# A decoder layer on one core: new first and last batches of the attention, and a closing stage whose loads are issued in the stage before it

## The chip, the cores and the metric

One core of one Trainium2 chip runs the whole program in one launch. The metric is the device time of one execution in microseconds (us), the median of several. A profile is taken of one execution; its span runs from the first to the last recorded work, and the execution's own time is a little longer than its span.

## What is computed

The input is x with 8 batches of 256 tokens of 512 features, float32, and a context of the same shape. Three residual blocks follow one another:

```
x = x + attention(layernorm(x))      # 16 heads of 32; each query sees 26 first and 64 last keys
x = x + convolution(ctx, ctx, layernorm(x))   # causal convolution of products of the context
x = x + ffn(layernorm(x))            # 12 experts, each token goes to its best 3
# ffn, closing part, for each batch:
#   pooled = mean over the 256 tokens of the experts' sum
#   phi    = sigmoid(relu(pooled @ Wp1 + bp1) @ Wp2 + bp2)
#   out    = sum * (1 - 0.8 * (phi > 0.7))
```

## The kernel before, in words

The kernel is five stages one after the other: attention, convolution, route, experts, finish. Each stage is a block with its own program for every engine, and a stage starts when all engines have left the one before. Inside a stage the order of work on an engine is written out by hand, and engines wait for each other on counted semaphores. TensorE is called PE below, VectorE is DVE, ScalarE is ACT, GpSimd is POOL, SyncE is SP.

**Attention.** A tile is 128 tokens, and a batch has two (t = 0, 1). All of x stays in SBUF as `xs`. SP loads x in four quarters of 1 MB each (L214), then the four weight matrices of 1 MB (L216), then small tables. ACT issues the load of the constants and, right behind it, those of the four biases. DVE computes the layer norm's statistics of all 16 tiles (L384, L387), ACT takes a square root (L231), DVE inverts it, and only then `normalise(0, 0)` starts (L403), whose result PE transposes (L528). Projections of batch 0 follow (L551). `kp`, the taps of the convolution, gets its diagonal from DVE after `add_bias(0, 3)`, is written out by SP, and ACT waits for that (`pad_out`) before it begins `batch(0)`.

`batch(b)` is software-pipelined: on PE it is scores of tile 0 (L571), projections of batch b+1, transposes of the probabilities `p_t` (L579), scores of tile 1, `p_v` (L592), the output product `w_o` (L560), and so on; transposes of the second layer norm's result of batch b-1 (`n_t`) lie between. ACT computes the exponentials, one instruction for each head (L258), and evacuates PSUM: `evac_pt` (L267), `evac_o` (L276), `evac_n` (L272). DVE does the row maxima (L423), the division of the probabilities (L433), biases, residual and statistics. The scores of tile 1 write the same four PSUM banks as those of tile 0 and the transposed probabilities, so they wait until tile 0 is through. In the last batch there is nothing of a next batch to fill the gaps; the order is otherwise the same.

**Experts.** 59 tiles of 128 gathered tokens go through two products. ACT scales a tile's result into `y` (L1548), POOL adds the expert's bias (L1478), copies the tile's indices (L1480), executes three short instructions that let earlier ones settle (L1455), and issues an indirect DMA that adds `y` into `acc` in DRAM (L1488). POOL waits for the last of these before the stage may end. SP loads the experts' weights, and at its end `x2`, the residual.

**Finish.** SP issues eight loads of `acc` into `o` (L1684), one per batch; ACT issues loads of the gate's weights. PE sums each batch over its tokens by a product with a column of ones, `pool_half(h)` for four batches (L1723), with two products per batch, one for each tile; the trace counts two MATMUL records for each float32 product here. Then the gate, `gate_half(h)`: transposes (L1730), hidden layer (L1736), output (L1742), with ACT and DVE between. PE does half 0's sums and gate, then half 1's. DVE then multiplies and adds the residual, eight instructions per half (L1770), and SP stores a batch when its two are done (L1688).

Of the kernel before, what the change touches and what calls it, by code (L numbers as in the profile page):

```python
# [14 lines left out]
P = 128  # L15
B, S, D = 8, 256, 512
KD = D // P
# [79 lines left out]
def attention(nc, xs, cst, x, wqT, wkT, wvT, woT, bq, bk, bv, bo, consts, qe, taps, diag, kpad):  # L97

    with ExitStack() as ctx:
# [35 lines left out]
        power = sb("power", [P, TPB])  # L135
# [5 lines left out]
        ps_t = psum("ps_t", [P, 512])  # L141
        ps_p = psum("ps_p", [P, 2, 512])
        ps_s = psum("ps_s", [P, 4, 512])
        ps_o = psum("ps_o", [P, KD, P])

        x_in = [sem(f"x_in{i}") for i in range(4)]
# [17 lines left out]
        pt_evac = sem("pt_evac")  # L164
        pv_done = sem("pv_done")
# [45 lines left out]
        def _(sp):  # L211
            xt = x.rearrange("b (t p) d -> p (b t) d", p=P)
            for i in range(4):
                sp.dma_start(xs[:, 4 * i:4 * i + 4, :], xt[:, 4 * i:4 * i + 4, :]).then_inc(x_in[i], 16)  # L214
            for w, src, s in ((wq, wqT, wq_in), (wk, wkT, wk_in), (wv, wvT, wv_in), (wo, woT, wo_in)):
                sp.dma_start(w[:].rearrange("p (k n) -> p k n", k=KD),  # L216
                             src.rearrange("(k p) n -> p k n", p=P)).then_inc(s, 16)
# [8 lines left out]
        def _(act):  # L226
            act.dma_start(cst[:], consts).then_inc(c_in, 16)
            for t, src in ((bias_q, bq), (bias_k, bk), (bias_v, bv), (bias_o, bo)):
                act.dma_start(t[:], src.partition_broadcast(P)).then_inc(b_in, 16)
            act.wait_ge(var_ready, 1)  # L230
            nc.scalar.activation(rstd[:], rstd[:], ACT.Sqrt).then_inc(std_ready, 1)  # L231
# [22 lines left out]
            def exps(b, t):  # L254
                for f in range(2):
                    act.wait_ge(nmx_ready, 4 * b + 2 * t + f + 1)
                    for s in range(8 * f, 8 * f + 8):
                        last = nc.scalar.activation(pm[:, t, s * NK:(s + 1) * NK],  # L258
                                                    ps_s[:, s // 4, (s % 4) * NK:(s % 4 + 1) * NK], ACT.Exp,
# [49 lines left out]
            batch(B - 1, True, False, True)  # L309
            evac_n(B - 1)  # L310

        @block.gpsimd
        def _(pool):
# [29 lines left out]
            def inverse_std(b):  # L343
                pool.wait_ge(var1_ready, b + 1)
                nc.gpsimd.tensor_tensor(rstd1[:], rstd1[:], power[:], ALU.pow).then_inc(rstd1_ready, 1)
# [18 lines left out]
            pool.wait_ge(power_ready, 1)  # L364
            pool.wait_ge(c_in, 16)
            first = Steps(pool, pool_step)
            for j in range(3):
                rope(0, j, first)
            batch(0, False, False)
# [9 lines left out]
        def _(dve):  # L379

            for i in range(4):
                dve.wait_ge(x_in[i], 16)
                with dve.Fori(4 * i, 4 * i + 4) as t:
                    nc.vector.bn_stats(stats[:, t], xs[:, t]).then_inc(stats_done, 1)  # L384
            dve.wait_ge(stats_done, NT)
            for t in range(NT):
                nc.vector.bn_aggr(mv[:, t], stats[:, t]).then_inc(aggr_done, 1)  # L387
            dve.wait_ge(aggr_done, NT)
            steps = Steps(dve, dve_step)
            nc.vector.tensor_scalar(rstd[:], mv[:, :, 1], EPS, None, ALU.add).then_inc(var_ready, 1)  # L390
            dve.wait_ge(std_ready, 1)
            steps.do(nc.vector.reciprocal(rstd[:], rstd[:]))
            dve.wait_ge(b_in, 64)
# [25 lines left out]
            def softmax_top(b, t, steps):  # L419
                dve.wait_ge(s_done, 2 * b + t + 1)  # L420
                for f in range(2):
                    sc = view(ps_s[:], f * 1024, [[512, 2], [NK, 4], [1, NK]])
# [4 lines left out]
            def softmax_sum(b, t, steps):  # L427
                for f in range(2):
# [78 lines left out]
            batch(B - 1, True, False, True, tail)  # L507
# [5 lines left out]
        def _(pe):  # L513
# [50 lines left out]
            def scores(b, t):  # L564
# [1312 lines left out]
```

## Time and profile before

| | us |
|---|---|
| median of 3 runs | 1565.55 |
| lowest, highest | 1563.95, 1566.26 |
| the profiled execution's own time | 1563.66 |
| its span | 1561.5 |
| what lies around the span | 2.2 |

The profile's times count from the start of the span. PE is the busiest engine with 1396.8 us. Busy time of another engine matters only where PE, or the end of the program, waits for it.

### The profile page before, as it was taken

To read this page: it belongs to the slowest core of one execution; us is meant where nothing else is said; L and a number is where in the kernel's file an instruction comes from. 1 tells how busy PE (TensorE), PEld (TensorE's weight loads), DVE (VectorE), ACT (ScalarE), POOL (GpSimd) and SP (SyncE) were. 2 spreads that over 40 slices of the span, in tenths; PEclk is the share of its full clock that TensorE was granted. 3 is DMA by queue.
4 is the path that set the end of the run, shared out by engine and by line. 5 is a ranking of instruction groups with operands and counts; after the bars stand their busy time and mean duration, and the time that the engine had idled before them with its cause. 6 is when DMAs were issued, how large, how long until landed. Compare 5 with 4: busy or idle time off the path is not lost. (4 is left out here: it accounts for less than half of the span.)

```text
span 1561.5 us, 27353 instructions
## 1 busy us (share of the span) xinstructions
PE 1396.8 (89%) x7656; PEld 1080.8 (69%) x7657; DVE 783.9 (50%) x1075; ACT 680.7 (44%) x1847; POOL 862.8 (55%) x989
## 2 busy tenths in 40 slices
PE   3899999769999526999999999999999999999956
PEld 1455555447777315888888888888888888888842
DVE  3455665539999687474434717446462552000003
ACT  0555555523444422444444444444444444445420
POOL 1544445324456305767676767767676766656530
PEclk9999999879999757999999999999999999999987
DMA  7000000015333333554444535444453543332115
GB/s 254 3 1 0 0 0 1 1 43 208 94 112 111 142 141 102 128 158 111 114 102 106 144 68 144 122 121 121 127 140 74 136 110 71 86 89 34 27 32 217
DMA packets 75461, 148.20 MB, mean 95 GB/s; under 512 B 9056, under 2 KB 13664, under 8 KB 74912
## 3 DMA queue, kind: packets, MB, share of 16 engines
q1 hardware_dynamic: 59424, 110.36, 22.7%
q0 software_dynamic: 14320, 35.40, 11.5%
q10 hardware_dynamic: 1680, 1.97, 0.4%
q8 instruction: 20, 0.33, 0.1%
q14 instruction: 17, 0.14, 0.0%
HBM read 115.11 MB, written 32.59 MB: 95 GB/s over the span
## 5 line engine op out<-in xcount | busy, mean ns | idle before, releaser
L1427 DVE TENSOR_TENSOR w_lo<-stage,w_hi 128x512 f32 x220 | 236.3, 1074 | 27.0
L1597 PE MATMUL ps_h<-w_hi,xh 128*128 x708 | 247.1, 361 | 1.5 <-ACT xh L1523 1.4
L1598 PE MATMUL ps_h<-w_lo,xh 128*128 x708 | 242.2, 354 | 0.0
L1620 PE MATMUL ps_y<-w_hi,hh 128*128 x590 | 237.0, 402 | 4.4 <-issue 4.4
L1621 PE MATMUL ps_y<-w_lo,hh 128*128 x590 | 231.9, 393 | 0.0
L1471 POOL TENSOR_TENSOR hl<-h,hh 128x1280 fp32r<-128x1280 f32 x59 | 191.8, 3250 | 12.4 <-ACT hh L1542 12.4
L1478 POOL TENSOR_TENSOR y<-y,b_sb 128x512 f32<-128x512 f32 x59 | 78.8, 1336 | 214.1 <-ACT y L1548 214.1
L1529 ACT ACTIVATE h<-ps_h 128x512 f32<-128x512 f32 x177 | 80.6, 527 | 214.3 <-POOL hl L1471 206.5
L933 PE MATMUL ps_b<-kv,toe 128*128 128x288 f32 x640 | 160.9, 412 | 12.7 <-POOL kv L800 6.8
L1602 PE MATMUL ps_h<-w_hi,xl 128*128 x708 | 164.1, 354 | 0.0
L1538 ACT ACTIVATE h<-ps_td,b_now 128x128 f32<-128x128 f32 x590 | 158.6, 391 | 3.9 <-PE ps_td L1610 1.2
L933 PEld LDWEIGHTS ps_b<-kv,toe 128*128 128x128 f32 x640 | 122.3, 193 | 47.5 <-DMA toe<-kpad 9.9
L1548 ACT ACTIVATE y<-ps_y,wt 128x512 f32<-128x512 f32 x59 | 40.6, 688 | 258.7 <-PE ps_y L1624 258.7
L1597 PEld LDWEIGHTS ps_h<-w_hi,xh 128*128 128x128 f32 x708 | 133.6, 189 | 22.2 <-issue 2.1
L1598 PEld LDWEIGHTS ps_h<-w_lo,xh 128*128 128x128 f32 x708 | 133.7, 189 | 20.3
L1624 PE MATMUL ps_y<-w_hi,hl 128*128 x590 | 144.9, 392 | 0.0
L1425 DVE CAST w_hi<-stage 128x512 f32 x220 | 134.3, 610 | 6.5 <-DMA stage<-in_wcat 6.0
L1602 PEld LDWEIGHTS ps_h<-w_hi,xl 128*128 128x128 f32 x708 | 119.8, 188 | 19.0
L1620 PEld LDWEIGHTS ps_y<-w_hi,hh 128*128 128x128 f32 x590 | 111.5, 189 | 26.7 <-issue 4.6
L1624 PEld LDWEIGHTS ps_y<-w_hi,hl 128*128 128x128 f32 x590 | 110.8, 188 | 24.4
L1621 PEld LDWEIGHTS ps_y<-w_lo,hh 128*128 128x128 f32 x590 | 111.6, 189 | 22.5
L1436 DVE TENSOR_TENSOR turn<-wt 128x1 f32<-128x1 f32 x11 | 3.3, 301 | 236.8 <-PE ps_h L1602 236.8
(213 smaller groups left out, 2315.7 us busy)
## 6 DMA issues: line engine op xcount, KB each, us to landing
stage<-in_wcat SPq DMA_DIRECT2D x220, 256.0 KB, 3.0
toe<-kpad SPq DMA_DIRECT2D x32, 256.0 KB, 3.4
cc<-in_ctx_rev SPq DMA_DIRECT2D x32, 192.0 KB, 3.5
w_lo<-in_wcat SPq DMA_DIRECT2D x4, 1280.0 KB, 11.9
acc<-added_c POOLq DMA_DIRECT2D x1, 4352.0 KB, 16.7
xs<-in_x SPq DMA_DIRECT2D x4, 1024.0 KB, 13.7
x2d<-xs SPq DMA_DIRECT2D x16, 256.0 KB, 2.9
xnd<-xn_c SPq DMA_DIRECT2D x16, 256.0 KB, 2.5
```

Of the source, the lines that this page charges most:

```text
L933: last = nc.tensor.matmul(view(ps[:], (4 * par + l) * 512, [[SPAN, B], [1, NPAIR]]), toe[:, par, (l - m) * P:(l - m + 1) * P], kv[:, buf, ...
L1425: nc.vector.tensor_copy(hi, stage[:, c % NSTAGE]).then_inc(w_rounded, 1)
L1427: nc.vector.tensor_tensor(lo, stage[:, c % NSTAGE], hi.bitcast(F32), ALU.subtract).then_inc(split_done, 1)
L1471: nc.gpsimd.tensor_tensor(hl[:], h[:], hh[:].bitcast(F32), ALU.subtract).then_inc(hl_ready, 1)
L1529: nc.scalar.activation(h[:, lo:hi], ps_h[:, c, 0:hi - lo], ACT.Copy).then_inc(h_evac, 1)
L1538: last = nc.scalar.activation(h[:, k * P:(k + 1) * P], ps_t[:, k // 4, (k % 4) * P:(k % 4 + 1) * P], ACT.Relu, bias=b1_now[:, k:k + 1])
L1597: nc.tensor.matmul(out, x_hi, part(w_hi, e, k * FF + lo, hi - lo), start=(k == 0), stop=False)
L1598: nc.tensor.matmul(out, x_hi, part(w_lo, e, k * FF + lo, hi - lo), start=False, stop=False)
L1602: last = nc.tensor.matmul(out, xl[:, k * P:(k + 1) * P], part(w_hi, e, k * FF + lo, hi - lo), start=False, stop=(k == KD - 1))
L1620: nc.tensor.matmul(ps_y[:], h_hi, part(w_hi, e, KD * FF + k * D, D), start=(k == 0), stop=False)
L1621: nc.tensor.matmul(ps_y[:], h_hi, part(w_lo, e, KD * FF + k * D, D), start=False, stop=False)
L1624: last = nc.tensor.matmul(ps_y[:], hl[:, k * P:(k + 1) * P], part(w_hi, e, KD * FF + k * D, D), start=False, stop=(k == KF - 1))
```

## The change

Three parts.

**The attention's start.** x is loaded in four parts of 1, 1, 2 and 4 batches, and between them the weights: x of batch 0, wq, x of batch 1, wk, wv, x of batches 2 and 3, wo, x of batches 4 to 7. The biases are issued after the constants have landed. Statistics are computed part by part: batch 0, then its normalisation; batch 1, then its own; batches 2 and 3 between `add_bias(0, 1)` and `add_bias(0, 2)`; batches 4 to 7 between `add_bias(0, 2)` and `add_bias(0, 3)`. The square root on ACT and the reciprocal on DVE are replaced by a power on POOL (three times: 2, 2 and 12 columns).

**The attention's end.** The eight PSUM banks become one tensor. In the last batch the scores of tile 1 go to the four banks of the other buffers right after those of tile 0; ACT runs the exponentials of tile 1 without waiting for tile 0's transposes; DVE evacuates the last transposed probabilities (`take_pt`) instead of ACT.

**The closing.** The eight loads of the sums and those of the gate's weights are issued by SP inside the experts' stage, into space of `w_lo` that is free by then; SP waits for the last indirect DMA itself. The last tile's bias is added by DVE. For every tile the copy of the indices comes first; the short settling instructions are left out for the last three. In `finish` DVE adds the two tiles of a batch (`add_pair`), and PE needs one product per batch instead of two; the result goes to a new buffer `g`.

```diff
-            for i in range(4):
-                sp.dma_start(xs[:, 4 * i:4 * i + 4, :], xt[:, 4 * i:4 * i + 4, :]).then_inc(x_in[i], 16)
...
+            load_x(0)
+            load_w(wq, wqT, wq_in)
+            load_x(1)
+            load_w(wk, wkT, wk_in)
+            load_w(wv, wvT, wv_in)
+            load_x(2)
+            load_w(wo, woT, wo_in)
+            load_x(3)
...
             act.dma_start(cst[:], consts).then_inc(c_in, 16)
+            act.wait_ge(c_in, 16)
...
-            act.wait_ge(var_ready, 1)
-            nc.scalar.activation(rstd[:], rstd[:], ACT.Sqrt).then_inc(std_ready, 1)
...
-            batch(B - 1, True, False, True)
-            evac_n(B - 1)
+            b = B - 1
+            exps(b, 0)
+            exps(b, 1, (0,), 0)
+            evac_pt(b, 0)
+            exps(b, 1, (1,), 0)
+            evac_o(b, 0)
+            evac_n(b - 1)
+            evac_o(b, 1)
+            evac_n(b)
...
+            def first_std(n, lo, hi):
+                pool.wait_ge(var_ready, n + 1)
+                r = rstd[:, lo:hi]
+                nc.gpsimd.tensor_tensor(r, r, power[:, lo:hi], ALU.pow).then_inc(std_ready, 1)
...
+            stats_of(0)
+            variance_of(0, TPB)
+            dve.wait_ge(std_ready, 1)
             normalise(0, 0)
             normalise(0, 1)
+            stats_of(1)
+            variance_of(TPB, 2 * TPB)
+            dve.wait_ge(std_ready, 2)
             normalise(1, 0)
             normalise(1, 1)
-            for j in range(4):
-                add_bias(0, j, bank_qkv0[j])
+            dve.wait_ge(b_in, 64)
+            add_bias(0, 0, bank_qkv0[0])
+            add_bias(0, 1, bank_qkv0[1])
+            stats_of(2)
+            add_bias(0, 2, bank_qkv0[2])
+            stats_of(3)
+            variance_of(2 * TPB, NT)
+            add_bias(0, 3, bank_qkv0[3])
+            dve.wait_ge(std_ready, 3)
...
+            def take_pt(f):
+                dve.wait_ge(pt_done, 4 * B - 1 + f)
+                if f == 0:
+                    dve.wait_ge(pv_done, 2 * B - 1)
+                nc.vector.tensor_copy(view(pT[:], f * 8 * P, [[4 * P, 2], [1, 4 * P]]), ps_s[0:NK, 2 * f:2 * f + 2])\
+                    .then_inc(pt_evac_last, 1)
+
+            b = B - 1
+            softmax_top(b, 0, tail)
+            softmax_top(b, 1, tail, 0)
+            variance(b - 1)
+            softmax_sum(b, 0, tail)
+            softmax_sum(b, 1, tail, (0,))
+            normalise_1(b - 1)
+            take_pt(0)
+            softmax_sum(b, 1, tail, (1,))
+            take_pt(1)
+            residual(b, 0, True, tail)
...
+            b = B - 1
+            scores(b, 0)
+            scores(b, 1, four_banks_free, 0)
+            p_t(b, 0, 0)
+            p_t(b, 0, 1)
+            pe.wait_ge(exp_done, 4 * b + 3)
+            p_v(b, 0)
+            pe.wait_ge(pt_evac, 4 * b + 2)
+            p_t(b, 1, 0)
+            n_t(b - 1, 0)
+            pe.wait_ge(exp_done, 4 * b + 4)
+            w_o(b, 0, True)
+            pe.wait_ge(pt_evac, 4 * b + 3)
+            p_t(b, 1, 1)
+            n_t(b - 1, 1)
+            p_v(b, 1, True)
+            w_o(b, 1, True)
...
-            sp.wait_ge(x2_in, 16 * HALVES)
+            for dst, src in end_small:
+                sp.dma_start(dst, src).then_inc(small_in, 16)
+            sp.wait_ge(added, 16 * NTILE)
+            sums = acc.rearrange("(t p) d -> p t d", p=P)
+            for b in range(B):
+                sp.dma_start(o[:, TPB * b:TPB * (b + 1)], sums[:, TPB * b:TPB * (b + 1)]).then_inc(o_in[b], 16)
...
+            i = NTILE - 1
+            e = dve.value_load(eid[0:1, i:i + 1], min_val=0, max_val=E - 1)
+            dve.wait_ge(b2_ready, E)
+            dve.wait_ge(y_evac, i + 2)
+            nc.vector.tensor_tensor(y[:, i % 2], y[:, i % 2], view(b2_sb[:], (e % 2) * D, [[1, D]]), ALU.add)\
+                .then_inc(y_ready, 1)
...
-                    for t in range(TPB):
-                        last = nc.tensor.matmul(ps_pool[0:BH, h], cst[:, at:at + BH], o[:, TPB * b + t],
-                                                start=(b % BH == 0 and t == 0), stop=(b % BH == BH - 1 and t == TPB - 1))
+                    last = nc.tensor.matmul(ps_pool[0:BH, h], cst[:, at:at + BH], pair[:, b],
+                                            start=(b % BH == 0), stop=(b % BH == BH - 1))
...
+            def add_pair(b):
+                dve.wait_ge(o_in[b], 16)
+                nc.vector.tensor_tensor(pair[:, b], o[:, TPB * b], o[:, TPB * b + 1], ALU.add).then_inc(paired, 1)
```

## Rows read from the trace of the kernel before

**Rows 1.** First line of the page: the span.

```profile
span 1561.5 us, 27353 instructions
```

**Rows 2.** Timeline of the attention's first 61 us: start, duration, engine, line.

```profile
8.51 2.47 DVE L384 BATCH_NORM_STATS2 stats<-xs  x4 [8.39 <-DMA xs<-in_x]
...
21.92 1.17 DVE L387 BATCH_NORM_AGGREGATE mv<-stats 128x2 f32<-128x6 f32 x16
...
24.56 1.09 PE L528 MATMUL ps_t<-cst,xn 128*128 128x128 f32 x4 [24.56 <-DVE xn L403]
...
27.45 9.51 PE L551 MATMUL ps_p<-wq,xT 128*128 128x512 f32 x16
...
52.94 1.28 ACT L258 ACT_TABLE_LOAD   x1
...
54.23 0.34 ACT L258 ACTIVATE pm<-ps_s,nmx 128x90 f32<-128x90 f32 x1
...
60.65 1.08 PE L579 MATMUL ps_s<-cst,pm 128*90 128x128 f32 x8 [0.42 <-DVE pm L433]
```

**Rows 3.** DMA issues of the first 25 us: KB each, us to landing.

```profile
bias_o<-in_L_attn_bo ACTq DMA_DIRECT2D x1, 256.0 KB, 9.6
...
cst<-in_consts ACTq DMA_DIRECT2D x1, 388.0 KB, 5.1
```

**Rows 4.** Stretches of 1 us: engines' busy time, PEclk, DMA share, GB/s.

```profile
27.00:28.00 1.00, 1.00 (x5) 0.79 (x4) 0.30 (x1) 0.30 (x2) 0.00 (x0) 1.00 1.04 406
28.00:29.00 1.00, 1.00 (x2) 0.34 (x1) 0.24 (x1) 0.57 (x2) 0.00 (x0) 1.00 0.84 301
```

**Rows 5.** Tile `kpad` in the attention: landing of its store.

```profile
DMA to landing us min/median/max: 1.7/1.7/1.7
```

**Rows 6.** Groups of POOL by shape: count, busy us, mean ns.

```profile
L345 POOL TENSOR_TENSOR rstd<-rstd,power 128x2 f32<-128x2 f32 x8 | 5.6, 705 | 92.9 <-DVE rstd L452 92.9
```

**Rows 7.** Timeline of the attention's last batch.

```profile
293.51 1.14 PE L571 MATMUL ps_s<-kT,qT 32*128 32x90 f32 x32
...
302.72 1.02 ACT L267 ACTIVATE pT<-ps_s 90x1024 f32<-90x1024 f32 x1 [0.67 <-PE ps_s L579]
...
309.30 3.67 PE L560 MATMUL ps_p<-wo,oT 128*128 128x512 f32 x8 [0.81 <-ACT oT L276]
...
315.45 1.08 PE L579 MATMUL ps_s<-cst,pm 128*90 128x128 f32 x8 [1.02 <-DVE pm L433]
...
317.64 1.08 PE L592 MATMUL ps_o<-pT,vv 90*32 90x128 f32 x32 [1.11 <-ACT pT L267]
...
319.53 3.67 PE L560 MATMUL ps_p<-wo,oT 128*128 128x512 f32 x8 [0.81 <-ACT oT L276]
```

**Rows 8.** A stretch of 100 us of the experts' stage.

```profile
1300.00:1400.00 100.00, 100.00 (x526) 85.05 (x525) 0.44 (x1) 47.58 (x117) 63.06 (x81) 1.00 0.32 77
```

**Rows 9.** Costliest groups: busy, mean ns, then idle time before it and its releaser.

```profile
L1478 POOL TENSOR_TENSOR y<-y,b_sb 128x512 f32<-128x512 f32 x59 | 78.8, 1336 | 214.1 <-ACT y L1548 214.1
```

**Rows 10.** Timeline from the last expert tile to the closing stage's first loads.

```profile
1510.05 1.26 POOL L1478 TENSOR_TENSOR y<-y,b_sb 128x512 f32<-128x512 f32 x1 [6.61 <-ACT y L1548]
...
1512.14 1.58 POOL L1488 DMA_INDIRECT acc<-y,si  x1
...
1519.34 4.25 SPq L1684 DMA_DIRECT2D o_sb<-acc  x8
```

**Rows 11.** DMA issues from 1500 us on: the last addition into `acc`.

```profile
acc<-y,si POOLq DMA_INDIRECT x1, 4.8
```

**Rows 12.** The chain that ended last: start, duration, what.

```profile
1523.37 9.06 PE ps_pool L1723 x16
...
1537.03 8.67 PE ps_pool L1723 x16
...
1547.13 2.83 PE ps_hid L1736 x16
...
1551.61 0.03 issue
1551.64 0.23 DVE z L1759
```

More of the change, by code:

```diff
@@ L139, in attention @@
         kp = pT[0:SH, 0:KPAD]
[L141 to L146, printed above, removed]
+        bank = psum("bank", [P, 8, 512])
+        ps_t = bank[:, 0]
+        ps_o = bank[:, 1].rearrange("p (k n) -> p k n", k=KD)
+        ps_p = bank[:, 2:4]
+        ps_s = bank[:, 4:8]
+        X_PARTS = ((0, 1), (1, 2), (2, 4), (4, B))
+        x_in = [sem(f"x_in{i}") for i in range(len(X_PARTS))]
         c_in, wq_in, wk_in, wv_in, wo_in, b_in = (sem(n) for n in ("c_in", "wq_in", "wk_in", "wv_in", "wo_in", "b_in"))
@@ L252, in evac_k, with exps @@
                 evac(qkt_done, 3 * b + 3, kT[:], ps_t[:].rearrange("p (k n) -> p k n", k=KD)[:, :, 0:NK])
-            def exps(b, t):
-                for f in range(2):
+            def exps(b, t, halves=(0, 1), at=4):
+                for f in halves:
                     act.wait_ge(nmx_ready, 4 * b + 2 * t + f + 1)
@@ L425, in softmax_top, with softmax_sum @@
                                             ALU.mult).then_inc(nmx_ready, 1)
[L427 to L428 removed]
+            def softmax_sum(b, t, steps, halves=(0, 1)):
+                for f in halves:
                     dve.wait_ge(exp_done, 4 * b + 2 * t + f + 1)
@@ L581, in p_t, with p_v @@
                 last.then_inc(pt_done, 1)
-            def p_v(b, t):
-                pe.wait_ge(pt_evac, 4 * b + 2 * t + 3)
+            def p_v(b, t, last=False):
+                if last and t:
+                    pe.wait_ge(pt_evac_last, 2)
+                else:
+                    pe.wait_ge(pt_evac, 4 * b + 2 * t + 3)
                 if t == 0:
@@ L1331, in experts @@
 def experts(nc, cst, w_hi, w_lo, stage, stage_in, split_done, wcat, b2, b2_sb, b2_in, b2_ready, b1_sb, xnd, x2d, x2,
-            x2_in, acc, first, tabs):
+            x2_in, acc, first, end, tabs):
     gidx, sidx, wt, eid, tstart_i, wexp = tabs
     gi, xg, gi_ready, g_in = first
+    o, o_in, end_small, small_in = end
     with ExitStack() as ctx:
@@ L1643, in _, with finish @@
                 tile(i, i // 2, i % 2, i + 1 < NTILE, i + 2 < NTILE)
-def finish(nc, cst, x2, x2_in, acc, wp1, bp1, wp2, bp2, out):
-    PH = wp1.shape[1]
-    KP = PH // P
+def finish(nc, cst, x2, x2_in, end, gate, out):
+    o, o_in, end_small, small_in = end
+    wp1_sb, bp1_sb, wp2_sb, bp2_sb = gate
+    KP = bp1_sb.shape[1]
     with ExitStack() as ctx:
@@ L1681, in _ @@
         def _(sp):
-            src = acc.rearrange("(t p) d -> p t d", p=P)
-            for b in range(B):
-                sp.dma_start(o[:, TPB * b:TPB * (b + 1)], src[:, TPB * b:TPB * (b + 1)]).then_inc(o_in[b], 16)
             dst = out.rearrange("b (t p) d -> p (b t) d", p=P)
@@ L1803, in decoder_layer @@
                 x2 = w_hi[:, 0, 0:NT * D].bitcast(F32).rearrange("p (t d) -> p t d", d=D)
+                o = w_lo[:, 0, 0:NT * D].bitcast(F32).rearrange("p (t d) -> p t d", d=D)
+                spare = w_lo[:, 0, NT * D:WS].bitcast(F32)
+                wp1, bp1, wp2, bp2 = (a[f"L0_ffn_{n}"] for n in ("Wp1", "bp1", "Wp2", "bp2"))
+                PH = wp1.shape[1]
+                KP = PH // P
+                gate = (spare[:, 0:KD * PH].rearrange("p (k n) -> p k n", k=KD), spare[:, KD * PH:KD * PH + KP],
+                        spare[:, KD * PH + KP:KD * PH + 2 * KP], spare[:, KD * PH + 2 * KP:KD * PH + 2 * KP + 1])
+                end_small = ((gate[0], wp1.rearrange("(k p) n -> p k n", p=P)), (gate[1], bp1), (gate[2], wp2),
+                             (gate[3], bp2.partition_broadcast(P)))
+                end = (o, [late.enter_context(nc.semaphore(f"o_in{b}")) for b in range(B)], end_small,
+                       late.enter_context(nc.semaphore("small_in_e")))
                 with ExitStack() as busy:
@@ L1818, in decoder_layer @@
                     experts(nc, cst, w_hi, w_lo, stage, stage_in, split_done, a["wcat"], a["L0_ffn_b2"], b2_sb, b2_in,
-                            b2_ready, b1_sb, xnd, x2d, x2, x2_in, acc, first, tabs)
-                finish(nc, cst, x2, x2_in, acc, a["L0_ffn_Wp1"], a["L0_ffn_bp1"], a["L0_ffn_Wp2"], a["L0_ffn_bp2"], out)
+                            b2_ready, b1_sb, xnd, x2d, x2, x2_in, acc, first, end, tabs)
+                finish(nc, cst, x2, x2_in, end, gate, out)
 def const_table():
```

133 lines of the change are left out of this document (73 added, 60 removed).

## The prediction

> **What bounds the kernel now.** I read first the page with its span and shares [rows 1], then the stretches of the experts' stage. There PE is busy 100.00 of 100 us at full clock [rows 8], and the change touches that stage only at its end, so nothing of its some 900 us can come or go unless an order in its loop is disturbed. What is left are the places where the change acts: the first 61 us, the last 38 us of the attention, and what follows the last expert tile. Stages follow one another behind barriers, so a gain at one place passes to the end whole, unless a later transfer takes it back.
>
> In the timeline of the start PE does nothing before 24.56 us: DVE computes all 16 tiles' statistics first [rows 2]. In the last batch of the attention PE stands in gaps between exponentials and transposes [rows 7]. After the last expert tile come the indirect DMA, a barrier, eight loads, and then a chain that is nearly all PE: two groups of 16 records for the sums, 9.06 and 8.67 us, and the gate behind each [rows 10, 12].
>
> **Part 1, the start.** When does PE begin? Batch 0's x is 0.52 MB instead of 1.05. The stream runs at about 0.406 MB/us [rows 4], the first quarter was in by 8.51 [rows 2] while biases shared the engines; half the bytes and no biases put the landing at about 6.1. The constants land 5.1 us after their issue [rows 3], so they are not late. Then two statistics at 2.47/4 = 0.62, two aggregations at 1.17/16 = 0.07, the small addition 0.2, and the power on POOL, 0.71 by its mean for 2 columns [rows 6] and 0.25 to wake it, then 0.6 for the first normalisation: 3.2 us. With 0.4 for waits PE starts at 9.7 in place of 24.56: a shift of 14.85 us, if everything that batch 0 needs arrives.
>
> wq is next in the queue: 1.57 MB of SP's queue and 0.4 of constants at 0.406 MB/us are through by about 9, and it is used at 27.45 - 14.85 = 12.6. wk and wv follow at 15 and 18, long before use. The biases are issued 5 us later than now, one landed 9.6 us after issue [rows 3]; the last lands near 18.6, and the first is used about 18.7. I take 0 and keep 1 us as its bound.
>
> The late item is x of batches 4 to 7. All the bytes are the same, so they are in when they are now, in the slice after 28 us [rows 4]; I take 29.7 with completion. DVE does their 8 statistics (5.0), 12 aggregations (0.9) and the addition (0.2) in front of `add_bias(0, 3)`: 35.8. The power of 12 columns: the row has 2 columns, and I take the same 0.7 with 0.25 of waking [rows 6]; if it grew with columns it would be 6 x 0.7 = 4.2, 3.5 us more. Then the tap's diagonal at 37.0, the store of `kpad` 1.7 [rows 5], 38.8. Behind that store ACT waits; queued there are the two copies of batch 1's x (1.0) and the first exponentials. They start at 39.85 against 54.23 now. From the first exponential to the second group of transposes on PE it is 60.65 - 54.23 = 6.42 [rows 2], so that group starts at 46.3; PE alone would have allowed 60.65 - 14.85 = 45.8. The gain is 60.65 - 46.3 = **14.3 us**.
>
> In this I leave out the table load of 1.28 us that now stands at 52.94, between the copies and the first exponential [rows 2]. It is there because the square root's table is in; after it no load follows although the later stages use copies, identity, relu and exponentials, so one table serves them all, and without the square root it can be loaded at the beginning, while ACT waits for PE. If it stays where it is, 1.3 us are lost: 13.0. The Trainium skill, "ScalarE: Activation LUTs", section "What ACT_TABLE_LOAD costs", counts a drain of 1380 ns on top of the 1283 ns of the load. By it a kept load would cost 2.7, not 1.3. The trace does not bear this out, since the first exponential starts at 54.23, 1.29 after the load's start.
>
> Bounds of the start: PE's own 14.85 above; below, the load kept, a power that grows with its columns, or statistics slowed beside POOL's rope, 10.
>
> **Part 2, the attention's last batch.** Scores of tile 0 stay at 293.51, those of tile 1 follow at once (1.14 each [rows 7]). ACT now has work without gaps from 297.0: 16 exponentials at 0.31 (5.1), 8 of tile 1 (2.5), two evacuations of 1.02 [rows 7] (2.1), 8 more (2.5), `evac_o` 0.6. So tile 0's `w_o` starts at 309.9 in place of 309.30, 0.6 later. But behind its 3.67 us PE has the last transposes at 313.5, which now start at 315.45. DVE evacuates them; no row has this copy on DVE, its bounds are 1.0 (ACT's time for it) and 1.4, I take 1.2. `p_v` then starts at 315.85 instead of 317.64, and from there to the stage's end all is as now, last `w_o` included (319.53 - 317.64 = 1.9 after it). Gain **1.8 us**. If PE's clock is down during `w_o`, whose 3.67 us are at the upper level, 3 us are lost; if DVE's order is smoother than I think, 1 more is won. Bounds: -1.5 and 3.
>
> **Part 3, the closing.** The last `y` is ready at 1509.8. POOL's 1.26 for the bias, 0.2 for the copy and 0.5 for three short ones [rows 10] are replaced by DVE's addition, 0.7 as for other additions of 512 columns: the indirect DMA is issued at 1510.8 instead of 1512.14, 1.35 earlier. It lands 4.8 later [rows 11], 1515.6. Now 2.4 us go by from landing (1516.94) to the first load (1519.34); afterwards SP waits for the landing itself, so it issues at 1515.7: 3.65 earlier. SP's eight issues take 4.25 [rows 10], and only then can the stage end. With 0.5 for the barrier (bound: the 2.4 of now), DVE's small copy 0.3 and `add_pair(0)` 0.7, PE starts at 1521.5, not 1523.37. The loads land every 1.3 us from 1519.7 on and are not late; the additions hide behind PE's products, which last 1.7 per batch while the clock is low.
>
> Half 0 has 8 records instead of 16. Of the 9.06 us the first five took 0.85 each (1.2 GHz), the other eleven 0.43 (2.4 GHz). Eight are 5 x 0.85 + 3 x 0.43 = 5.4, end 1526.9. The gate from 1532.43 to 1537.03 is 4.6: 1531.5. Half 1, of 8.67 us with four records at the lower clock, keeps these and loses 8 at 0.43 or so: 5.0, end 1536.5. The gate from 1545.70 to 1551.64 is 5.9: DVE's z at 1542.4 instead of 1551.64 [rows 12]. From there to the end nothing changes. That is 9.2; for lags at the added hand-over I take off 0.3: **8.9 us**. Bounds: 3.5 (below) and 10.
>
> The settling instructions and the earlier copy of the indices cost and save nothing in the loop: POOL waits 214.1 us for `y` over 59 tiles, 3.6 each [rows 9].
>
> **Sum.** 14.3 + 1.8 + 8.9 = 25.0 us. The profiled execution took 1563.66 (span 1561.5 [rows 1] and 2.2 around it): 1538.7. It was 1.9 under the median of the runs, so the same gain on 1565.55 gives **1540.5**, which I predict.
>
> **Rivals.**
>
> *The clock in the closing.* Half the products means half the work that keeps PE busy. PE's records are at 1.2 GHz in 1523 to 1527, after idle time, and again in the second gate, whose 2.83 us [rows 12] are longer than the 1.93 of the first. If all stayed at 1.2 GHz: half 0 +1.3, first gate +1.3, half 1 8 x 0.85 = 6.8 or +1.8, second gate +1: 5.4 less, gain 19.6, time 1546. For it: more of the stage is waiting. Against: 5.4 us of unbroken products are longer than the 3.9 after which the clock rose. The Trainium skill, "TensorE: Matmul & The Clock Gate", section "Part 1: The HAM clock gate", says that "the default state is throttled, and activity releases the throttle", which speaks for this rival. Chance 0.17.
>
> *The start is held by the late x.* Statistics of the last 8 tiles run beside POOL's rope, the power grows with its columns, or the table load stays: together or alone 2 to 5 us, gain 20 to 23 or, with one more on top, 16; 1543 to 1549. Against: the rope should be over by 32.5. Chance 0.18.
>
> *Nothing at the start.* If transfers did not finish in the order of the queue, batch 0's x could land as late as the quarters do, over 14 us, and the start gains 4 or so: total 15, 1551. The first quarter was in by 8.51, with the others queued. Chance 0.04.
>
> *Slower.* The loop of 59 tiles has a new order on POOL. To turn 25.0 us into a loss each tile would have to lose 25.0/59 = 0.42 us on PE, and more than 0.47 for slower by 0.2%. POOL has 3.6 us of slack a tile, so its reordering would have to hold the next `hl` back by more than 4; then 0.5 a tile makes 1570. Nothing in the trace shows it. Chance 0.02.
>
> **Chances.** Forecast 0.58 (its own range 1537.5 to 1543.5), clock 0.17, late x 0.18, no order 0.04, slower 0.02, no change at all 0.01. 0.2% is 3.1 us, about what a measurement of this kernel can tell from no change: faster 0.96, same 0.02, slower 0.02. The range reaches from the upper bounds of the parts (14.85 + 3 + 10 = 27.9, 1537.7) with a little for the spread of the runs, 1537, to the clock and late x cases, 1548.5.
>
> **What would show it.** The first transposes at 9.7; first exponential at 39.9 and no table load in front; the attention ends 16.1 us earlier; SP's first load of `acc` at once behind the landing; 8 records in each sum, three of the first group at 0.43. The prediction is wrong if the gap in front of the first exponential is over 3 us on ACT, if PE's sums are all at 0.85, or if the experts' stage is longer than before.

## The result and the profile after

The changed kernel takes 1538.37 us (median of 4 runs, 1537.53 to 1541.13); the kernel before, run with it, 1565.02 (4 runs, 1563.95 to 1566.26). The ratio is 0.9832 with a 95% interval of [0.9815, 0.985]: 26.65 us less. The forecast was 1540.5 in a range of 1537.0 to 1548.5, a gain of 25.0. The profiled execution took 1537.53, its span is 1535.5 against 1561.5 [rows 1], 26.0 less.

First lines of the page after:

```profile
span 1535.5 us, 27262 instructions
...
PE 1389.0 (90%) x7640; PEld 1079.4 (70%) x7641; DVE 778.3 (51%) x1087; ACT 677.0 (44%) x1843; POOL 861.1 (56%) x981
```

PE is busy 7.8 us less than the 1396.8 of before, so most of the 26.0 us, some 18, is idle time of PE that is gone. The same 100 us of the experts' stage as in [rows 8], start and end, then the engines' busy time, the granted clock and the DMA's share:

```profile
1300.00:1400.00 100.00, 100.00 (x526) 85.05 (x525) 0.00 (x0) 47.27 (x116) 62.03 (x78) 1.00 0.34 84
```

PE is still without a gap there at full clock, so in these 100 us the new order of POOL's instructions costs nothing; the whole stretch of the 59 tiles is compared below, under what was given back.

**The start.** Timeline of the first 50 us (start, duration, engine, line), which answers to [rows 2]:

```profile
5.55 1.29 DVE L416 BATCH_NORM_STATS2 stats<-xs 128x6 f32<-128x512 f32 x2 [5.44 <-DMA xs<-in_x]
...
7.29 1.28 ACT L259 ACT_TABLE_LOAD   x1 [7.16 <-issue]
...
8.95 1.09 PE L591 MATMUL bank<-cst,xn 128*128 128x128 f32 x4 [8.95 <-DVE xn L433]
...
29.51 4.84 DVE L416 BATCH_NORM_STATS2 stats<-xs 128x6 f32<-128x512 f32 x8 [4.64 <-DMA xs<-in_x]
...
35.64 2.29 POOL L390 TENSOR_TENSOR rstd<-rstd,power 128x12 f32<-128x12 f32 x1 [4.53 <-DVE rstd L423]
...
37.96 0.15 DVE L540 TENSOR_TENSOR pT<-pT,dd 32x1 f32<-32x1 f32 x1 [1.88 <-POOL rstd L390]
...
39.83 0.39 ACT L259 ACTIVATE xkT<-bank 128x256 f32<-128x256 f32 x1 [5.28 <-DMA kpad<-pT]
...
40.59 0.34 ACT L272 ACTIVATE pm<-bank,nmx 128x90 f32<-128x90 f32 x1
...
47.02 1.08 PE L645 MATMUL bank<-cst,pm 128*90 128x128 f32 x8 [1.47 <-DVE pm L463]
```

PE starts 15.6 us earlier (8.95 for 24.56), but the second group of transposes only 13.63 (47.02 for 60.65). Read upwards from that row, with the brackets telling how long an engine stood idle and what released it: the exponentials, ACT's wait of 5.28 for the store of `kpad`, the diagonal, the power of 12 columns, and eight statistics that waited 4.64 for x. No table load stands in front of the exponentials; the only one is at 7.29, before ACT's first work.

**The attention's last batch**, same view, which answers to [rows 7]:

```profile
278.39 2.04 PE L637 MATMUL bank<-kT,qT 32*128 32x90 f32 x64
...
294.38 3.67 PE L623 MATMUL bank<-wo,oT 128*128 128x512 f32 x8 [0.52 <-ACT oT L290]
...
298.96 1.22 DVE L555 COPY pT<-bank 90x1024 f32<-90x1024 f32 x1 [2.81 <-PE bank L645]
...
300.24 1.08 PE L661 MATMUL bank<-pT,vv 90*32 90x128 f32 x32 [0.88 <-DVE pT L555]
...
302.13 3.67 PE L623 MATMUL bank<-wo,oT 128*128 128x512 f32 x8 [0.81 <-ACT oT L290]
```

Counted from the scores, the last `w_o` starts after 23.74 us, where it was 26.02.

**The closing.** Timeline from the last `y` on, which answers to [rows 10]:

```profile
1493.48 0.69 ACT L1657 ACTIVATE y<-ps_y,wt 128x512 f32<-128x512 f32 x1 [9.04 <-PE ps_y L1733]
1494.45 0.69 DVE L1548 TENSOR_TENSOR y<-y,b_sb 128x512 f32<-128x512 f32 x1 [210.36 <-ACT y L1657]
1495.88 1.57 POOL L1597 DMA_INDIRECT acc<-y,si  x1 [8.30 <-issue]
1500.53 3.99 SPq L1513 DMA_DIRECT2D w_lo<-acc  x8
...
1505.91 5.19 PE L1821 MATMUL ps_pool<-g_sb,cst 128*4 128x512 f32 x8 [12.47 <-DVE g_sb L1856]
```

And the chain that ended last, which answers to [rows 12]:

```profile
1512.55 1.93 PE ps_hid L1834 x16
...
1515.71 5.24 PE ps_pool L1821 x8
...
1522.38 1.93 PE ps_hid L1834 x16
...
1525.58 0.23 DVE z L1861
```

From the issue of the indirect DMA to the first load it is 4.65 us instead of 7.20, each group of sums has 8 records, and the second gate's hidden layer lasts 1.93 instead of 2.83.

### The profile page after: what moved, and what is told of

It is laid out like the page before. It is cut to its first block and busy times, and to the rows that moved or that the text cites. A ratio compares the mean times of both kernels' runs of the same rounds, so it can differ in the third digit from the quotient of the medians.

```text
span 1535.5 us, 27262 instructions
## 1 busy us (share of the span) xinstructions
PE 1389.0 (90%) x7640; PEld 1079.4 (70%) x7641; DVE 778.3 (51%) x1087; ACT 677.0 (44%) x1843; POOL 861.1 (56%) x981
## 5 line engine op out<-in xcount | busy, mean ns | idle before, releaser
L1524 DVE TENSOR_TENSOR w_lo<-stage,w_hi 128x512 f32 x220 | 231.6, 1053 | 27.0
L1575 POOL TENSOR_TENSOR hl<-h,hh 128x1280 fp32r<-128x1280 f32 x59 | 184.8, 3132 | 15.8 <-ACT hh L1651 15.7
L1522 DVE CAST w_hi<-stage 128x512 f32 x220 | 127.5, 579 | 7.9 <-DMA stage<-in_wcat 7.4
```

Source lines behind the costliest of these rows:

```text
L1522: nc.vector.tensor_copy(hi, stage[:, c % NSTAGE]).then_inc(w_rounded, 1)
L1524: nc.vector.tensor_tensor(lo, stage[:, c % NSTAGE], hi.bitcast(F32), ALU.subtract).then_inc(split_done, 1)
L1575: nc.gpsimd.tensor_tensor(hl[:], h[:], hh[:].bitcast(F32), ALU.subtract).then_inc(hl_ready, 1)
```

## Experiments

**The three parts, each undone.** Each of the first three is the changed kernel with one part as before, with five runs each beside a median of 1563.6 us (9 runs) for the kernel before.

Start undone:

```diff
-        X_PARTS = ((0, 1), (1, 2), (2, 4), (4, B))
+        X_PARTS = ((0, 2), (2, 4), (4, 6), (6, B))
...
-            act.wait_ge(c_in, 16)
...
-            stats_of(0)
-            variance_of(0, TPB)
+            for i in range(4):
+                stats_of(i)
+            variance_of(0, NT)
+            steps.do(nc.vector.reciprocal(rstd[:], rstd[:]))
```

> The changed kernel with the attention's start put back (x in quarters ahead of the weights, biases at once, all statistics first, square root on ScalarE and reciprocal on VectorE); its end and the closing stay changed. Theory, parts add: the start is worth 13.6 to 15.1 us of the 26.0 in the traces, so about 11 to 12.5 remain, 1565.0 - 12 = 1553. Rival, the start's gain is partly eaten later (2.2 us vanish between the attention's end and the last tile): then undoing it costs only 11 to 12 us, 1550. First transposes at 24.6 us, second group of probability transposes of batch 0 near 60.6.

Last batch undone:

```diff
-            exps(b, 0)
-            exps(b, 1, (0,), 0)
...
+            batch(B - 1, True, False, True)
+            evac_n(B - 1)
```

> The changed kernel with the last attention batch in the order of the kernel before (ordinary batch, ScalarE evacuates everything); start and closing stay changed. Theory: the new order is worth 2.7 us on TensorE's path from the last batch's first scores to the stage's end (36.06 us with it, 38.78 without), so 1538.4 + 2.7 = 1541.1. Rival: part of the 2.7 us is the clock's phase and not the order; then the time is within 1.5 us of the changed kernel.

Closing undone:

```diff
-            sp.wait_ge(added, 16 * NTILE)
-            sums = acc.rearrange("(t p) d -> p t d", p=P)
-            for b in range(B):
-                sp.dma_start(o[:, TPB * b:TPB * (b + 1)], sums[:, TPB * b:TPB * (b + 1)]).then_inc(o_in[b], 16)
+            sp.wait_ge(x2_in, 16 * HALVES)
...
+                settle(2)
...
-                    last = nc.tensor.matmul(ps_pool[0:BH, h], cst[:, at:at + BH], pair[:, b],
+                    for t in range(TPB):
```

> The changed kernel with the experts' end and the closing stage put back whole. Theory: from the last tile's y to the end before took 52.4 us and after 42.0, so the closing is worth 10.4 us: 1538.4 + 10.4 = 1548.8. Rival, the clock: 1.3 us of these come from the second gate, which ran at the full clock after and not before, and could as well fall the other way: 1547.5.

| | median (5 runs) | ratio, 95% | the part is worth, of 1565 us |
|---|---|---|---|
| start undone | 1550.79 | 0.9911 [0.9897, 0.9924] | 12.4 |
| last batch undone | 1540.98 | 0.9848 [0.9835, 0.9862] | 2.5 |
| closing undone | 1548.89 | 0.9906 [0.989, 0.9922] | 11.6 |

The last column is the difference to the ratio 0.9832, times 1565. Both ratios have an interval of some 0.0015 either way, so each entry is uncertain by some 3 us, and by the medians alone the last batch is not told from nothing. The sum is 26.5, the whole 26.3: within that the parts add up. The start undone came out at 1550.79, at the expectation's rival (1550) and not at its 1553. In the traces the stretch of each part can be taken alone: from the start to the last batch's scores 292.64 us with the start undone and 278.39 changed, 14.25; the last batch 38.80 and 36.06, 2.74; from the last `y` to the second `z` 42.53 and 32.10, 10.43.

What such a stretch varies by shows in the other traces, where its program is the same. The last batch in the new order takes 36.02 to 36.89 in eleven traces, 38.78 and 38.80 in the two with the old order, so the order is worth 1.9 to 2.8 us. The closing takes 32.10 to 32.15 in five of the six traces that leave it as changed, and 34.81 in the sixth (weights last, below).

**What holds the first exponential.** Two variants look at this; they and the four after them were run once each. Runs of one kernel lie up to 5 us apart (1562.90 to 1567.41 for the kernel before), so what follows is read from stretches of the traces. The first variant puts the square root back, three times, with the reciprocal on DVE:

```diff
+            def root(n, lo, hi):
+                act.wait_ge(var_ready, n + 1)
+                nc.scalar.activation(rstd[:, lo:hi], rstd[:, lo:hi], ACT.Sqrt).then_inc(std_ready, 1)
...
-            first_std(2, 2 * TPB, NT)
...
+            steps.do(nc.vector.reciprocal(rstd[:, 2 * TPB:NT], rstd[:, 2 * TPB:NT]))
```

> The changed kernel, but the three powers on GpSimd are square roots on ScalarE with a reciprocal on VectorE again (2, 2 and 12 columns); order of loads and of statistics stay new. Theory: the square root brings its table with it, so a load of 1.28 us stands again in front of the first exponential, behind batch 1's copies; the diagonal is added about 1.3 us earlier, because 12 columns of square root and reciprocal take 0.5 us and the power took 2.3. The two cancel: first exponential 40.4 to 40.9, against 40.59. Rival, a switch of tables costs 2.66 us: 41.8 or later. Rival, the load is not tied to the square root: no load, first exponential at 39.3.

1539.54 us, span 1537.6. Its timeline:

```profile
35.75 0.21 ACT L249 ACTIVATE rstd<-rstd 128x12 f32<-128x12 f32 x1 [0.96 <-DVE rstd L427]
...
36.23 0.21 DVE L545 RECIPROCAL rstd<-rstd 128x12 f32<-128x12 f32 x1
36.48 0.15 DVE L547 TENSOR_TENSOR pT<-pT,dd 32x1 f32<-32x1 f32 x1
...
39.83 1.28 ACT L277 ACT_TABLE_LOAD   x1
...
41.12 0.34 ACT L277 ACTIVATE pm<-bank,nmx 128x90 f32<-128x90 f32 x1
```

Root and reciprocal (0.21 each) bring the diagonal 1.5 us earlier than the power of 2.29, ACT is through its wait for the store 0.9 earlier (38.94 for 39.83), and the table load of 1.29 takes more than that back: the first exponential is 0.53 later than in the changed kernel, just outside the expected 40.4 to 40.9. Two things besides the root differ here: the last part of x was usable at 29.72, not 29.51, and the store of `kpad` took 2.3 us, not 1.7. Power in place of the root is thus worth half a microsecond or less in this trace, not the load's 1.3. The drain that the Trainium skill ("ScalarE: Activation LUTs", "What ACT_TABLE_LOAD costs") puts on top of the load does not show here either: the exponential starts 1.29 after the load's start.

The second takes the diagonal, and so the store of `kpad`, out from behind the power; DVE waits for the power only before it normalises batch 2:

```diff
+                if isinstance(b, int) and b == 0:
+                    dve.wait_ge(std_ready, 3)
...
+            dve.wait_ge(taps_in, 32)
+            nc.vector.tensor_tensor(kp[:, P - 1:P], kp[:, P - 1:P], dd[:], ALU.add).then_inc(pad_ready, 1)
             variance_of(2 * TPB, NT)
             add_bias(0, 3, bank_qkv0[3])
-            dve.wait_ge(std_ready, 3)
-            dve.wait_ge(taps_in, 32)
-            nc.vector.tensor_tensor(kp[:, P - 1:P], kp[:, P - 1:P], dd[:], ALU.add).then_inc(pad_ready, 1)
```

> The changed kernel, but VectorE adds the taps' diagonal right behind the last statistics, ahead of their aggregation, and waits for the power of 12 columns only before it normalises batch 2. Theory: what holds the first exponentials is the late part of x, then aggregation, power (2.3 us) and diagonal, 3.6 us of which now leave the path; the first exponential starts near 37.3 instead of 40.59, but TensorE is in projections till 44.5, so the second group of transposes moves only from 47.02 to about 45.4, and the whole gains 1.5 us. Rival, TensorE's stream binds: the second group stays within 0.3 us of 47.0.

1536.92 us, span 1534.8. Its timeline:

```profile
34.24 0.13 DVE L539 TENSOR_TENSOR pT<-pT,dd 32x1 f32<-32x1 f32 x1
...
37.35 0.34 ACT L272 ACTIVATE pm<-bank,nmx 128x90 f32<-128x90 f32 x1
...
43.69 1.91 PE L646 MATMUL bank<-cst,pm 128*90 128x128 f32 x16
```

The exponentials start 3.24 us earlier, and both groups of transposes run back to back from 43.69, right when PE is through with the query projection of batch 1. The second group is some 2.4 us earlier (it starts about 0.9 into these 16), so PE binds from here and the rest of the 3.24 is lost behind it. Of the 2.4 some 0.8 is the clock's: PE is through with that projection at 43.69 here and at 44.47 in the changed kernel, where the granted clock rose at 38 us instead of 37. The diagonal's place itself is worth 1.6, as was expected. But the span is only 0.7 shorter: `w_o` of batch 6 lasts 5.37 us in this trace, as before the change, against 3.67 in the changed kernel's, 1.7 given back by the clock.

**Is it the order of the queue?** The same parts of x, all ahead of the weights:

```diff
-            load_x(0)
+            for i in range(4):
+                load_x(i)
...
-            load_x(1)
```

> The changed kernel with its statistics part by part, but all four parts of x are queued ahead of the four weights. Theory: transfers finish in the order of the queue; batch 0's transposes still start at 9.0, but wq lands at 21 to 22, so the query projections start there instead of 11.84 and the start loses 7 to 9 us net (the late x is early now, so no wait for it). Rival, the start's gain is that of the split statistics alone: the loss is under 3 us.

1549.47 us, span 1547.4. Its timeline:

```profile
9.02 1.09 PE L589 MATMUL bank<-cst,xn 128*128 128x128 f32 x4 [9.02 <-DVE xn L431]
...
22.32 8.96 PE L612 MATMUL bank<-wq,xT 128*128 128x512 f32 x16 [10.19 <-DMA wq<-in_L_attn_Wq]
...
1515.34 6.43 PE L1819 MATMUL ps_pool<-g_sb,cst 128*4 128x512 f32 x8 [12.72 <-DVE g_sb L1854]
```

Batch 0's x is as early as in the changed kernel, and PE still waits 10.19 us for wq. The last batch's scores come at 287.61, 9.2 later. So of the 14.25 us of the start 5.0 (292.64 - 287.61) can be had with x cut and the weights last; the other 9.2 need the weights in between. The span is longer by more, 11.9, and 2.7 of that lie in the closing, whose program was not touched: from the last `y` to the second `z` it takes 34.81 us here. Half 0's sums last 6.43 instead of 5.19, with the granted clock at 0.50 up to 1521, and the first gate's hidden layer 2.40 instead of 1.92.

**The closing, piece by piece.** Two products per batch again, without DVE's additions:

```diff
-                    last = nc.tensor.matmul(ps_pool[0:BH, h], cst[:, at:at + BH], pair[:, b],
+                    for t in range(TPB):
+                        last = nc.tensor.matmul(ps_pool[0:BH, h], cst[:, at:at + BH], o[:, TPB * b + t],
```

> The changed kernel, but VectorE adds no pairs: TensorE sums each batch with two products again. Loads stay in the experts' stage. Theory: 8 more records in each half, at 0.43 us most of them and with the first in place 0.7 us earlier: first load to z of the second half 25.05 + 3.4 + 3.4 - 0.7 = 31, so 6 us slower. Rival, the loads bind, since they land every 1.35 us and a batch's two products take 0.86 to 1.7: half 0 loses under 2 us, in all under 4.

1543.66 us, span 1541.5. Its timeline:

```profile
1500.50 3.98 SPq L1513 DMA_DIRECT2D w_lo<-acc  x8
...
1504.93 8.72 PE L1822 MATMUL ps_pool<-w_lo,cst 128*4 128x512 f32 x16 [11.65 <-PEq L1432]
...
1531.56 0.22 DVE L1861 TENSOR_SCALAR z<-ps_z,w_lo 128x4 f32<-128x4 f32 x1 [6.44 <-PE ps_z L1841]
```

From the first load to the second `z` it takes 31.06 us against 25.05: the addition on DVE is worth 6.0 net. Its own cost, already taken off in that, is 1.0 at the front: the first product starts 4.43 us after the first load without it and 5.38 with it.

The loads issued by `finish` as before, everything else changed:

```diff
-            sp.wait_ge(added, 16 * NTILE)
-            sums = acc.rearrange("(t p) d -> p t d", p=P)
-            for b in range(B):
-                sp.dma_start(o[:, TPB * b:TPB * (b + 1)], sums[:, TPB * b:TPB * (b + 1)]).then_inc(o_in[b], 16)
```

> The changed kernel, but the eight loads of the sums are issued at the head of the closing stage, as before; the pairs, the early gate weights and the last bias on VectorE stay. Theory: from landing of the last indirect DMA to the first load it is 2.4 us again instead of none, so from issue of that DMA to the first load 7.1 to 7.2 instead of 4.65; but the stage no longer has to wait for SP's eight issues, so the first product starts 4.0 + 0.7 = 4.8 behind the first load instead of 5.38. Net 1.9 us slower. Rival, the barrier is the same wherever the loads are: no difference.

1542.75 us, span 1540.6. Its timeline:

```profile
1497.48 1.57 POOL L1593 DMA_INDIRECT acc<-y,si  x1 [8.33 <-issue]
1504.47 4.02 SPq L1786 DMA_DIRECT2D w_lo<-acc  x8
...
1509.00 6.08 PE L1820 MATMUL ps_pool<-g_sb,cst 128*4 128x512 f32 x8 [13.95 <-DVE g_sb L1855]
...
1516.53 2.71 PE L1833 MATMUL ps_hid<-pooled_t,w_lo 128*128 128x4 f32 x16 [0.37 <-ACT pooled_t L1801]
```

From the issue to the first load 6.99 us instead of 4.65, but from there to the first product 4.53 instead of 5.38, since the stage's start is already over. The net 1.5 is what issuing early is worth for the waits. From issue to the second `z` the difference is 3.6 (33.28 against 29.70); the other 2.1 are PE's: sums 6.08 instead of 5.19 and a gate at the lower clock, 2.71 instead of 1.92. Here, as in the closing of the trace with the weights last, the clock rival of the prediction is seen at work, for 2 us of its 5.4.

The last bias on POOL as before:

```diff
-            nc.vector.tensor_tensor(y[:, i % 2], y[:, i % 2], view(b2_sb[:], (e % 2) * D, [[1, D]]), ALU.add)\
-                .then_inc(y_ready, 1)
...
-                if not (isinstance(i, int) and i == NTILE - 1):
```

> The changed kernel, but GpSimd adds the last tile's bias as well. Theory: y to issue of the last indirect DMA was 3.01 us before and is 2.40 with VectorE; with GpSimd's 1.26 us and without the settling instructions it is 0.92 + 1.26 + 0.2 = 2.4 to 2.6. So VectorE's part is worth 0.2 us or less, and the gain of 0.6 us comes from the short instructions and the copy that are gone. Rival: VectorE saves the difference of the two additions, 0.57 us, and this version needs 3.0.

1538.97 us, span 1536.9. Its timeline:

```profile
1494.51 0.69 ACT L1649 ACTIVATE y<-ps_y,wt 128x512 f32<-128x512 f32 x1 [9.04 <-PE ps_y L1725]
1495.42 1.26 POOL L1577 TENSOR_TENSOR y<-y,b_sb 128x512 f32<-128x512 f32 x1 [6.68 <-ACT y L1649]
1497.42 1.58 POOL L1589 DMA_INDIRECT acc<-y,si  x1 [0.73 <-issue]
```

From `y` to the issue it is 2.91 us; 3.01 before, 2.40 after. So DVE's addition gains 0.5, and the settling instructions and the copy, which no longer stand there, only 0.1: from the addition's end to the DMA it is 0.74 without them and was 0.83 with them [rows 10], and for 0.73 of it the profile shows nothing that POOL waits for. My expectation put all the time between addition and DMA on those instructions, and fell; its rival (3.0) was right.

**Can the clock be held up?** 13 products of no use, 26 records, put behind PE's last work of the experts' stage, into a bank that nobody reads then:

```diff
+            for _ in range(13):
+                nc.tensor.matmul(ps_h[:, 0], ident, cst[:, 0:512], start=True, stop=True)
```

> The changed kernel plus 13 idle products of 512 columns on TensorE at the end of the experts' stage, whose result nobody reads. Theory: TensorE falls to 1.2 GHz in the 12 us it waits, and the first half's products start there; kept busy it starts at 2.4 GHz, half 0's sums end 1.2 us earlier (then bound by the loads, one batch every 1.35 us), the whole 1 to 2 us earlier. Rival, the loads or VectorE's additions bind half 0 already: no gain.

1538.47 us (4 runs, 1537.08 to 1540.16), ratio 0.9832 [0.9817, 0.9847] beside 1565.01 (9 runs): no gain. Timeline:

```profile
1493.34 11.32 PE L1754 MATMUL ps_h<-cst 128*128 128x512 f32 x26
...
1506.07 2.76 PE L1823 MATMUL ps_pool<-g_sb,cst 128*4 128x512 f32 x6 [1.41 <-DVE g_sb L1858]
...
1511.64 2.82 PE L1836 MATMUL ps_hid<-pooled_t,w_lo 128*128 128x4 f32 x16 [0.37 <-ACT pooled_t L1804]
...
1516.04 5.18 PE L1823 MATMUL ps_pool<-g_sb,cst 128*4 128x512 f32 x8
```

The sums now run at 2.4 GHz and then wait for the additions, which follow the loads every 1.35 us. The granted clock falls after them, between 1512 and 1513, and most of the gate runs at 1.2: half 1's sums start 22.50 us after `y`, where the changed kernel has 22.16. In this trace the slow stretch was not removed but moved. The Trainium skill ("TensorE: Matmul & The Clock Gate", "Part 1: The HAM clock gate") holds that the throttled state is the default and activity lifts it; the sums agree with that (granted clock 1.00 from 1506 to 1510), and the gate right behind them shows that it was no lasting gain here.

**All that helped, together**: the diagonal first, wo behind the last part of x, and the 13 products.

```diff
-            load_w(wo, woT, wo_in)
             load_x(3)
+            load_w(wo, woT, wo_in)
...
+                    dve.wait_ge(std_ready, 3)
...
+            for _ in range(13):
```

> The changed kernel with the diagonal ahead of the aggregation, the last part of x queued ahead of wo, and TensorE kept busy before the closing. Theory: 1.5 to 2 us at the start and 1.2 to 2 at the end, 1535 against 1538.4. Rival: each of the two vanishes in the clock's phase, and the time is within 1.5 us of the changed kernel's.

1536.98 us (5 runs, 1535.01 to 1542.56), ratio 0.9833 [0.9816, 0.985]. Its span is 1532.9, 2.6 under that of the changed kernel. Its timeline:

```profile
27.27 4.84 DVE L416 BATCH_NORM_STATS2 stats<-xs 128x6 f32<-128x512 f32 x8 [2.13 <-DMA xs<-in_x]
...
37.68 0.34 ACT L272 ACTIVATE pm<-bank,nmx 128x90 f32<-128x90 f32 x1
...
44.41 1.91 PE L646 MATMUL bank<-cst,pm 128*90 128x128 f32 x16
```

x's last part is usable 2.2 us earlier, but then PE is the bound, and the transposes are no earlier than with the diagonal first alone. In this trace the 13 products are followed by sums and a first gate that are both at 2.4 GHz (hidden layer 1.92 us), and still the closing takes 31.91 us from `y` to the second `z`, 0.2 less than in the changed kernel: the sums wait for the additions, and these for the loads. So with the clock up it is the loads that bind half 0, as the rival for the 13 products had it. The runs do not tell this kernel from the changed one.

## Why the prediction was right, point by point

**The sum.** 14.3 + 1.8 + 8.9 = 25.0 was forecast. From the traces: 15.12 up to the last batch's scores, 2.72 in that batch, 10.41 from `y` to the second `z`, and 2.19 given back in between, in all 26.06. Some of these are no part of the change: 1.5 at the start, 0.44 in the last batch and 1.31 in the closing go with the clock, as shown below. Without them and without the 2.19 it is 13.63 + 2.28 + 9.1 = 25.0, the forecast to the tenth. The mechanisms were right, but that agreement is luck: single terms are off by up to 0.75 us either way and cancel, and the clock's 3.25 and the 2.19 nearly do.

**The start.** Each forecast stands first, what the trace shows behind it. PE at 9.7: 8.95, as batch 0's x was usable at 5.55, not 6.1. Late x at 29.7: 29.51. Statistics 5.0: 4.84. No table load: right. The power of 12 columns, taken as 0.7: 2.29, 1.6 more, the term that was mis-sized, within its bound of 4.2. This much of the rival "held by the late x" came true. First exponential 39.85: 40.59. Second transposes 46.3: 47.02, a gain of 13.63 for 14.3. That the late x holds the start was forecast; that x's late part through the power holds it above what PE needs is shown by the diagonal put first: 2.4 us in its trace, 1.6 at the changed kernel's clock. The further 1.5 up to the last batch come from the clock, not from a part of the change: `w_o` of batch 6 took 5.37 us before, with a granted clock of 0.68, and 3.67 after, with 1.00. Of the kernel before, then of the kernel after:

```profile
288.21 5.37 PE L560 MATMUL ps_p<-wo,oT 128*128 128x512 f32 x8 [0.81 <-ACT oT L276]
...
274.79 3.67 PE L623 MATMUL bank<-wo,oT 128*128 128x512 f32 x8 [0.81 <-ACT oT L290]
```

It takes 5.37 also with the late loads, whose program is the changed kernel's up to there, and 3.67 with the start undone. In all it is 5.37 in four of the thirteen traces and 3.67 in nine.

**The last batch.** `w_o` +0.6: +0.2. Copy on DVE 1.2: 1.22. Last `w_o` 1.9 us earlier after the scores: 2.28. The rest of the 2.72 is 0.44 behind it, where the first of the two last `n_t` takes 0.66 instead of 1.11, at a granted clock of 1.00 instead of 0.50. With the old order put back, the last `w_o` starts 26.02 us after the scores again, as before the change.

**The closing**, each stretch with its forecast gain and what the traces show:

| | forecast | shown |
|---|---|---|
| `y` to the issue of the indirect DMA | 1.35 | 0.61 |
| issue to the first load | 2.3 | 2.55 |
| first load to the first product | -1.8 | -1.35 |
| half 0 | 3.66 | 3.85 |
| first gate | 0 | 0.01 |
| half 1 | 3.67 | 3.43 |
| second gate | 0 | 1.31 |
| lags | -0.3 | |
| sum | 8.9 | 10.41 |

The first row is the step that was wrong in kind: the copy and the settling instructions were counted as 0.7 and are worth 0.1, since POOL takes 0.74 from the addition to the DMA with nothing between. The second gate is the one that was mis-sized: it was copied from before with its 2.83 us, and in the shorter chain it fell into a stretch of the upper clock (granted 1.00 instead of 0.64). The clock rival had it the other way round. It didn't come in the changed kernel; it came for 2 us when the loads were late, and for 2.7 in the trace with the weights last, whose closing is the changed kernel's to the instruction. So the same program can have it or not: it stayed away in five of the six traces of this closing, the profiled execution among them, and no run shows what decides it. That the second gate ran faster than before was luck.

**What was given back.** 2.19 us: 0.98 in the convolution's stage, 1.33 from the first expert product to the last `y`, and 0.12 gained in the route. The convolution and the route were not touched. From the attention's end to the first expert product the same program takes 267.03 us before and 267.89 after, and 266.99 to 268.65 in all thirteen traces. In the experts' stage POOL's instructions in the 59 tiles have a new order. From the first product to the last `y` it is 909.81 us before and 910.71 with the closing undone, which puts the old order back, and 910.16 to 912.03 in the eleven traces with the new order. So a cost of the new order of a few tenths of a microsecond is neither shown nor excluded; one of 2 us is not seen.

Stretches around the first expert product, the granted clock the third number from the end. Of the kernel before:

```profile
599.00:603.00 4.00, 3.68 (x10) 2.93 (x11) 2.54 (x1) 0.00 (x0) 3.84 (x3) 0.57 0.00 0
603.00:607.00 4.00, 4.00 (x22) 3.37 (x21) 3.08 (x3) 1.03 (x2) 3.73 (x2) 1.00 0.00 0
```

Of the kernel after:

```profile
582.00:586.00 4.00, 3.66 (x9) 2.90 (x10) 2.53 (x1) 0.01 (x1) 3.82 (x3) 0.50 0.00 0
586.00:590.00 4.00, 4.00 (x16) 3.23 (x15) 3.10 (x3) 0.60 (x1) 3.76 (x2) 0.81 0.00 0
```

PE starts from idle at 599.32 and 582.34; at first at 1.2 GHz in both, and the first 12 products take 4.30 and 5.25 us. In the convolution 40 us show 0.96 after the change (342 to 382) where the same 40 (360 to 400) show 1.00 before. Later in the same stage it is the other way round, 0.92 before (480 to 520) and 0.96 after (462 to 502). That is the same clock that gave 1.7 in batch 6. Together such stretches move a trace by 1 to 3 us either way, as much as the whole part of the last batch. That the start of a stretch against the clock is what decides it is argued from these rows; no run here set it on purpose.

**The signs of being wrong.** Three were named. PE's sums were not all at 0.85. The experts' stage did get longer, by 1.33 us from its first product to its last `y`; that sign was badly chosen, as traces of one order differ there by 1.9. And ACT does stand idle for 5.28 us, over the 3 us named, though in front of the two copies and not directly in front of the first exponential; the forecast itself had ACT wait there for the store. So two of the signs were met in their wording while the mechanism they stood for held.

## What to carry to other kernels

Where the first input holds the start, order the queue by first use: cutting x alone left PE waiting 10 us for a weight, and with the weights in between the start was worth 14 in the traces (12.4 by the medians). Sum each chain from the wait that ends last, and ask for each cheap instruction on it whether its size is the one that was measured: a power of 2 columns was no price for one of 12. On a chain of products with waits between them, halve the products on an engine that idles, and expect the clock to add or take an us or two.

## What the runs showed of the hardware that I had not expected

- POOL's power takes 0.71 us for 128x2 [rows 6] and 2.29 for 128x12: about 0.16 for each column more, by these two sizes. ACT's square root of 12 columns took 0.21, as for 2 columns (0.20).
- From POOL's addition to its indirect DMA it is 0.74 us with nothing between, 0.83 with a copy and three short instructions.
- A load that waits for the indirect DMA inside the stage starts 4.60 to 4.89 us after the issue (ten traces); one behind the stage's end 6.99 to 7.20 (three).
- The same product of the same size took 5.37 or 3.67 us (`w_o` of batch 6), in kernels that are the same up to there, with a granted clock of 0.68 or 1.00.
- 11.3 us of products of no use kept the next sums at 2.4 GHz. In one trace the gate after them fell to 1.2, in the other it did not; the closing took 32.33 and 31.91 us, against 32.10 without them.
- The closing of one and the same program took 32.10 to 32.15 us in five traces and 34.81 in a sixth.
